# Two quarters of a tile per program step in a fused attention and LoRA-mixture kernel

## The reference

```python
x = x + xattn(layernorm(x), ctx, ctx)      # x, ctx: (8, 512, 2048) float32
x = x + ffn(layernorm(x), router_w, A, B)
# xattn: 8 heads of 64 of the 512 channels; q = softmax over the channels of a head,
#        k = softmax over the 2048 positions; kvs = k.T @ v per head; out = q @ kvs
# ffn:   logits = x @ router_w.T (4 experts), the two best kept, softmax over them = gates
#        mid = x @ A.T (rank 16 per expert), delta = gates * (mid @ B.T) * 4
```

## Time and profile before

| what | value |
|---|---|
| median of 3 runs | 462.5 us (462.09 to 462.72) |
| the profiled execution | 461.86 us, its span 460.1 us |
| mean granted TensorE clock | 0.968 |
| PE, DVE, ACT, POOL busy | 94%, 82%, 69%, 78% of the span |
| moved by DMA | 137.55 MB, 299 GB/s |

### The profile page before, as it was taken

The page is one execution under the profiler, slowest core; times in us unless marked ns, Lnnn a source line. Parts: engine busy times, 40 slices in busy tenths (PEclk is TensorE's granted clock), DMA queues, the critical chain, the costliest instruction groups (busy, mean ns, idle before and its releaser), DMA issues.

```text
span 460.1 us, 16033 instructions
## 1 busy us (share of the span) xinstructions
PE 434.0 (94%) x6504; PEld 382.7 (83%) x6504; DVE 378.9 (82%) x1045; ACT 317.8 (69%) x436; POOL 358.7 (78%) x343
## 2 busy tenths in 40 slices
PE   6569998999999999999999999999999999999975
PEld 5458887888889888888888988888888988888854
DVE  2478778898998989898988989898989989775864
ACT  1266888795858777786858777786958687785320
POOL 0457999988898989898898988898888989894510
PEclk9658999999999999999999999999999999999997
DMA  8995997799999999999999999999999997445247
GB/s 288 420 410 187 310 274 266 261 285 322 347 285 355 327 342 345 312 336 320 339 305 323 338 361 334 323 326 328 355 291 345 300 366 256 172 170 184 93 182 275
DMA packets 38969, 137.55 MB, mean 299 GB/s; under 512 B 4208, under 2 KB 6384, under 8 KB 38768
## 3 DMA queue, kind: packets, MB, share of 16 engines
q1 hardware_dynamic: 38896, 136.52, 85.8%
HBM read 102.95 MB, written 33.55 MB: 297 GB/s over the span
## 4 chain that ended last, share of the span: by engine, by line
PE 80%; POOL 6%; DVE 4%; DMA 4%; issue 2%; ACT 2%; SPq 1%; POOLq 0%; DVEq 0%
PE num_ps L407 23%; PE kv_ps L390 15%; PE raw_ps L423 12%; PE delta_ps L478 11%; PE delta_ps L479 6%; PE kv_ps L438 5%; PE raw_ps L454 4%; DMA sq_a<-in_bt_dram 4%; POOL ek_sb L311 3%; POOL y_sb L323 3%; PE kv_ps L443 1%; PE raw_ps L464 1%; DVE max_n L632 1%; DVE y_sb L716 1%; PE kv_ps L375 1%
## 5 line engine op out<-in xcount | busy, mean ns | idle before, releaser
L311 POOL TENSOR_TENSOR ek_sb<-ctx_sb,kmax_row 128x512 f32<-128x512 f32 x128 | 167.6, 1311 | 35.7 <-ACT kmax_row L511 35.7
L323 POOL TENSOR_TENSOR y_sb<-attnT,y_sb 128x512 f32<-128x512 f32 x128 | 164.0, 1281 | 38.6 <-DVE attnT L707 38.5
L407 PE MATMUL num_ps<-kv_sb,x_sb 128*128 128x130 f32 x1024 | 140.8, 281 | 3.3 <-ACT kv_sb L563 2.0
L407 PEld LDWEIGHTS num_ps<-kv_sb,x_sb 128*128 128x128 f32 x1024 | 125.7, 192 | 6.2 <-ACT kv_sb L563 2.7
L716 DVE TENSOR_TENSOR y_sb<-delta_ps,y_sb 128x512 f32<-128x512 f32 x128 | 87.5, 684 | 23.3 <-PE delta_ps L479 22.1
L632 DVE TENSOR_REDUCE max_n<-ctx_sb 128x32 f32<-128x512 f32 x128 | 86.4, 677 | 10.6 <-DMA ctx_sb<-in_ctxt_dram 10.6
L390 PE MATMUL kv_ps<-ctx_sb,ek_sb 128*64 128x65 f32 x2048 | 93.2, 234 | 0.2 <-ACT ek_sb L533 0.2
L707 DVE TENSOR_TENSOR attnT<-num_ps,rden 128x512 f32<-128x512 f32 x128 | 88.5, 691 | 4.8 <-DVE rden L704 0.4
L390 PEld LDWEIGHTS kv_ps<-ctx_sb,ek_sb 128*64 128x64 f32 x2048 | 74.6, 140 | 17.8 <-issue 6.0
L533 ACT ACTIVATE ek_sb<-ek_sb 128x1024 f32<-128x1024 f32 x64 | 67.2, 1049 | 25.8 <-POOL ek_sb L311 25.7
L423 PE MATMUL raw_ps<-w_sb,y_sb 128*64 128x69 f32 x2048 | 84.4, 223 | 0.0
(11 more groups left out here) (67 smaller groups left out, 461.7 us busy)
## 6 DMA issues: line engine op xcount, KB each, us to landing
ctx_sb<-in_ctxt_dram SPq DMA_DIRECT2D x64, 520.0 KB, 5.6
x_sb<-in_x_dram SPq DMA_DIRECT2D x64, 512.0 KB, 6.1
y_sb<-in_xt_dram SPq DMA_DIRECT2D x64, 512.0 KB, 6.5
out_dram<-y_sb SPq DMA_DIRECT2D x60, 512.0 KB, 6.3
out_dram<-y_sb SPq DMA_DIRECT2D x8, 256.0 KB, 3.8
sq_a<-in_bt_dram SPq DMA_DIRECT2D x1, 1024.0 KB, 16.2
w_sb<-in_wt_dram SPq DMA_DIRECT2D x1, 552.0 KB, 10.1
cst<-in_consts_dram SPq DMA_DIRECT2D x1, 145.0 KB, 2.3
```

The costliest lines, as they stand in the source:

```text
L311: pool.tensor_tensor(ek_sb[:, t % 2, chunks(g), :].rearrange("p (a b) c -> p a b c", b=2), ctx_sb[:, t % 4, 2 * g:2 * g + 2, 1:P + 1, :].r ...
L323: pool.tensor_tensor(y, attnT[:, g, :], y, ALU.add).then_inc(x1_made, 1)
L407: mm = pe.matmul(num_ps[:, j // 2, at:at + 2 * (DH + 1)], x_sb[:, t % 4, c * P:(c + 1) * P], kv_sb[:, t % 2, :], start=True, stop=True, sk ...
```

## The change

Every engine's loop now goes over `q` in steps of 2, and each operation handles two quarters in one step. On TensorE the two `numerator` calls, which need the array as 128 columns, stand with the two `delta` calls, `sum_squares`, `turn_mid` and `spread_kmax` between them; then come both `kv`, then both `project` (64 columns), then `fold_squares` (32 columns). `delta_ps` is one pair of banks that both deltas of a step fill, and one `add_delta` of twice the width reads. `turn_max` writes into `delta_ps`, no longer into `num_ps`, so `delta` waits for `kmax_made` and `turn_max` for `out_made`. `max_part` handles 64 rows at a time. `fold_squares` adds the 16 blocks of squares into one block of 128 columns, so `copy_squares` copies 128 columns where it copied 384, and `sum_squares` is one matmul where it was three. Offsets grow by one where they were odd. The orders of VectorE, ScalarE and GpSimd are written anew.

```diff
@@ TensorE @@
-            for q in range(FIRST, LAST + 1):
+            for q in range(FIRST, LAST + 1, 2):
+                turn_max(tile_in(q, -4))
+                numerator(*tile_at(q, 6))
                 delta(*delta_at(q))
-                turn_max(q)
-                sum_squares(q)
-                if q == 1:
+                delta(*delta_at(q + 1))
+                sum_squares(tile_in(q, 12))
+                turn_mid(pair_in(q, 20))
+                if q == 2:
                     sum_w()
-                numerator(*tile_at(q, 5))
-                spread_kmax(q)
-                kv(*tile_at(q, 0))
-                project(*tile_at(q, 7))
-                fold_squares(q)
-                turn_mid(q)
+                spread_kmax(tile_in(q, -4))
+                numerator(*tile_at(q + 1, 6))
+                for k in range(2):
+                    kv(*tile_at(q + k, 0))
+                for k in range(2):
+                    project(*tile_at(q + k, 8))
+                fold_squares(tile_in(q, 10))
@@ delta @@
-                after(pe, out_made, 8 * p + i - 1)
+                if i % 2 == 0:
+                    after(pe, out_made, 4 * p + i // 2)
+                    after(pe, kmax_made, min((8 * p + i + 22) // 4 + 2, NT))
@@ VectorE @@
+            for q in range(FIRST, LAST + 1, 2):
+                a, b = pair_in(q, 16), pair_in(q, 18)
+                kv_recip(tile_in(q, 4))
+                max_whole(tile_in(q, -4))
+                ln1_mean(tile_in(q, -2))
+                normalise(*tile_at(q, 6))
+                add_delta(*delta_at(q))
+                normalise(*tile_at(q + 1, 6))
+                mid_low(pair_in(q, 20))
...
+                max_part(*tile_at(q, -8))
...
+                for k in range(2):
+                    bn_part(*tile_at(q + k, -4))
...
@@ add_delta @@
-                y = y_sb[:, pair_slots(p), 2 * i:2 * i + 2, :]
+                y = y_sb[:, pair_slots(p), 2 * i:2 * i + 4, :]
@@ SP, the last pair @@
-            for i in range(8):
-                sp.wait_ge(out_made, 8 * (NP - 1) + i + 1)
+            for i in range(4):
+                sp.wait_ge(out_made, 4 * (NP - 1) + i + 1)
                 store_last(i)
```

More of the change, by code:

```diff
@@ L120, in xattn_lora_moe_kernel @@
         num_ps = bank("num_ps", (P, 2, 512))
[L121 to L122 removed]
+        delta_ps = bank("delta_ps", (P, 2, 512))
+        max_ps = delta_ps[:, 0, 0:P]
         ctx_landed = [sem(f"ctx_landed{i}") for i in range(4)]
@@ L452, in sum_squares, with turn_mid @@
                 pe.wait_ge(sq_summed, t + 1)
-                for k in range(3):
-                    mm = pe.matmul(raw_ps[p % 2][:, odd, COL_SQ:COL_SQ + 2], sq_sum[:, t % 2, k, :], ones[:, 0:2],
-                                   start=False, stop=(k == 2), skip_group_check=True)
-                mm.then_inc(sq_done, 1)
-            def turn_mid(q):
-                p = pair_at(q, 15)
+                pe.matmul(raw_ps[p % 2][:, odd, COL_SQ:COL_SQ + 2], sq_sum[:, t % 2, :], ones[:, 0:2],
+                          start=False, stop=True, skip_group_check=True).then_inc(sq_done, 1)
+            def turn_mid(p):
                 if p is None:
@@ L808, in mid_low @@
                                   ALU.subtract).then_inc(lo_made, 1)
-            for q in range(FIRST, LAST + 1):
-                early = q < 0
-                if early:
-                    max_whole(q)
-                a, b, c = pair_at(q, 13), pair_at(q, 14), pair_at(q, 15)
-                if b is not None:
-                    gate_beats(b, 0)
-                if c is not None:
-                    gate_mid(c)
-                max_part(*tile_at(q, -8))
-                kv_recip(q)
+            for q in range(FIRST, LAST + 1, 2):
+                a, b = pair_in(q, 16), pair_in(q, 18)
[6 more added lines that the diff above has]
+                mid_low(pair_in(q, 20))
                 if a is not None:
@@ L823, in _ @@
                 if b is not None:
-                    gate_beats(b, 1)
-                    gate_mask(b)
-                mid_low(q)
-                bn_part(*tile_at(q, -5))
-                add_delta(*delta_at(q))
+                    gate_rank(b)
+                max_part(*tile_at(q, -8))
                 if a is not None:
                     gate_logits(a)
-                if b is not None:
-                    gate_rank(b)
-                if not early:
-                    max_whole(q)
-                normalise(*tile_at(q, 5))
-                if a is not None:
                     gate_below(a)
+                    gate_beats(a, 0)
+                    gate_beats(a, 1)
+                    gate_mask(a)
                 if b is not None:
```

183 lines of the change are left out of this document (83 added, 100 removed).

## The result

| | before | changed |
|---|---|---|
| median of 6 runs each, same chip | 462.47 us (461.86 to 462.72) | 467.79 us (467.01 to 468.67) |
| ratio to before, 95% interval | | 1.0117 (1.0102 to 1.0131) |
| span of the profiled execution | 460.1 us | 465.2 us |
| mean granted TensorE clock | 0.968 | 0.951 |

The change made the kernel 1.2% slower. I had forecast 0.4% faster, 460.7 us.

The account below looks back on a forecast made before the run. TensorE was taken to set the pace before the change. Start 87, 13 pairs of 25.0, 22.0 to the last fold and 24.6 behind it gave a 458.6 us span, forecast as 460.7 us; range 451 to 468, its own 453 to 461.5.

Parts of the forecast that it names:

- S: Moment VectorE begins a step's first normalise; the second numerator was to start 1.07 us later, TensorE standing about 0.3.
- step B: Second of a pair's four steps, with the gates' second half on VectorE; 6.45 us there, 6.5 by TensorE.
- the two lists: TensorE's and VectorE's work per step; the longer sets its length: 5.6, 6.5, 6.4, 6.5, together 25.0 us per pair.
- D: Fourth step of a pair, with two bn_stats, kv_recip and max_whole on VectorE: 6.1 us there, 6.5 by TensorE.
- second rival: Steady part: VectorE's lateness passed on through the one num_ps; slower, 468 us at a pair of 25.6; chance 0.30.
- Step C: Third step of a pair, with mid_low and two bn_stats; VectorE's list 6.1 us, 6.4 with deltas starting late.
- the guard: Deltas' wait for max_whole (kmax), since turn_max writes into delta_ps; deltas 0.3 us late after a step that fills VectorE.
- A: First step of a pair, with the gates' first half and ln1_mean; VectorE's list rules at 5.6 us.
- Start: Up to normalise 16: first normalise at about 38 us, steady part at 87 instead of 81.86, 5 us lost.
- End: Behind the last fold: one-copy delta_ps makes four rounds of 2.5 us each; 24.6 us counted, 21.0 before.
- Rival 1: Steady part: TensorE alone sets the pace, VectorE ready early; 443 to 445 us; chance 0.17.
- Rival 3: Whole kernel: steady part gains what start and end lose (5+1.7 us), at a pair of 25.1; 462 us; chance 0.16.

Follow-up runs that it names:

- e8: Changed kernel plus a needless one-input VectorE maximum over 256 columns, four per pair of tiles; 483.04 us, ratio 1.0443.
- e9: Kernel before plus the same needless one-input VectorE maximum over 256 columns, four per pair of tiles; 468.29 us, ratio 1.0133.
- e7: Changed kernel with maximum in the second delta bank, b_lo one step earlier, and two delta banks in turn for the last pair; 452.55 us, ratio 0.9787.
- e4: Kernel before with only the new squares: one block of 128 columns, one matmul in sum_squares instead of three; 456.49 us, ratio 0.987.
- e10: Changed kernel with the old squares: blocks of 384 and 128 columns, three matmuls in sum_squares; 480.86 us, ratio 1.0393.
- e1: Changed kernel with turn_max writing into the second bank of delta_ps, so only the second delta of a step waits for the maximum; 460.39 us, ratio 0.997.
- e3: Changed kernel with two delta_ps banks used in turn, 512-column additions and half-size stores, for the last pair alone; 462.20 us, ratio 1.0.
- e2: Changed kernel with the four b_lo pieces computed one step earlier on VectorE (q = 2, not 4); 466.03 us, ratio 1.0068.
- e11: Three-repair version (452.55 us) with both kv ahead of the second numerator and the wide maximum ahead of the second normalise; 459.04 us, ratio 0.9924.
- e5: Changed kernel plus a needless VectorE addition of 256 columns with two SBUF inputs, four per pair of tiles; 505.43 us, ratio 1.0942.
- e6: Kernel before plus the same needless VectorE addition of 256 columns, four per pair of tiles; 475.60 us, ratio 1.0285.

## Why the prediction was wrong

- **What bounds it, and the mechanism: right.** The wait of the second numerator for `attnT` arose where I put it, at S+0.97 in step B for my S+1.07, and a step lasts as long as the longer of the two lists. e8 against e9 shows that the changed kernel passes on nine tenths of VectorE's lateness, the one before under four tenths. It appears 33 times with 24.4 us, where I wrote some 50 times; in the steady part it stands in B and D only. My sign for the second rival, TensorE waiting more than 2 us per pair, did not come: PE stands 1.4.
- **The widths: right.** A wide addition lasted 1.22 us and a wide maximum 1.21; from start to start a maximum took 1.13, and the addition 1.14 where the next operation waited for nothing. The overhead of 0.07 in these terms came from no row. The runs bear it out: 0.33 for 256 columns (e8), 0.60 for 512, 1.13 for 1024.
- **TensorE's saving: somewhat smaller.** PE was busy for 23.69 us of a pair in e7, for my 23.3 (my terms, 25.65 less 1.4 and 0.8, add to 23.45). The squares took 0.7 us from it (24.92 in e4) for my 0.8, the new order 0.8 (e10) to 1.2 (e4 to e7) for my 1.4. What it was worth depended on the guard: nothing with it, 0.54 us per pair without (e1 against e4). That most of it would stay in the new wait was the right sentence; I still credited the pair with 0.64 us, and it was 0.43.
- **Step C and the guard: the term of the steady part that was mis-sized.** For the guard I took 0.3 us, in C alone. Against e1 it cost 0.48 there (6.74 for 6.26) and 0.13 in A, where I counted nothing for it: 0.6 per pair, twice what I had. Without the guard my lists give 24.7 per pair, and e1 shows 24.73, but by errors that cancel: C was 6.26 for my 6.1, where `ln1_var` (0.17) was not in my list, and B and D were 0.05 shorter each. So twelve pairs took 25.31 for my 25.0, and the last 23.95, which I had not foreseen; 12x0.31 less 1.05 are the 2.7 us by which the steady part missed.
- **Start: mis-sized.** I had 87 and it was 90.09. The first `normalise` (38.59 for my 38; `b_lo` took 3.5 us for 4.2, and the maximum ahead of it began 0.6 later than I had) and the first step (8.33 for 8.3) held. The second step took 6.81 for my 5.4, because the clock had fallen and I had given it the fast one; the six steps behind it took 36.4 for 35.6. The numerator of that second step shows the clock, in the timeline of PE:

```profile
47.89 2.10 PE L411 MATMUL num_ps<-kv_sb,x_sb 128*128 128x130 f32 x8
49.92 1.71 PE L395 MATMUL kv_ps<-ctx_sb,ek_sb 128*64 128x65 f32 x32
51.47 1.14 PE L427 MATMUL raw_ps<-w_sb,y_sb 128*64 128x69 f32 x32
```

  The 2.23 us in which PE stood before `spread_kmax` at 47.50, for `copy_kv`, cost little by themselves, as VectorE's S was at 46.92 and the numerator had to wait for it until about 47.9. But then the numerator took 2.03 us to the next start for 0.99, and both `kv` 1.55 for 0.98: 1.6 us, all of the excess of this step. These are places of one execution: in e3 and e8, whose start up to there is the same program, `normalise` 16 came at 91.4 and 91.3.
- **End: right in sum, by luck.** 24.6 forecast, 25.2 measured. The four last rounds took 2.53 at the fast clock and 3.39 at the slow one, and three of them had the slow one. I had named this ("up to 1 us per step") and left it out of the sum; three times 0.86 is 2.6 us. All else behind the last fold was 2 us shorter than the 14.6 that my sum leaves for it and that I had not split into terms. One part of it the rows show: from the end of the last addition to the end of the span it is 3.2 us, for 4.8 before, though the last store has twice the size. Why is not shown.
- **The sum.** 3.1 (start), 2.7 (pairs), 0.2 and 0.6 (end) are the 6.6 us between my 458.6 and the 465.2 of the span. A pair of 25.1 was the point from which I let the second rival decide, and 25.21 is beyond it; of its 468 only 2.7 of the 6.6 us came from there, though, and the rest from start and end, while I had worked it out from a pair of 25.6 alone. That its time came out is luck. My own last step was off as well: 460.4 and the 0.6 to the median are 461.0, not 460.7. The lists of B and D add to 6.33 and 6.03, for which I wrote 6.45 and 6.1; TensorE's 6.5 is longer, so the sum does not change.
- **Rival 1** (TensorE alone, 443 to 445) is refuted by the waits for `attnT` and by e8, in which work on VectorE alone made a pair 1.2 us longer. **Rival 3** (a pair of 25.1 that pays for start and end) had the right signs; start and end lost 10.7 us together (8.2 and 2.5), where it had 6.7.

The theory with which I went into the experiments stands: e7 got 15.2 us back, as much as the three places gave one by one. Its rival, that undoing one would only move the wait, holds for e2 in small (0.46 us of a new wait), and for e11.

What stays open: how much of e11's loss is the round trip and how much the keys, what the pads would cost without the guard, and why the old order passes on nearly four tenths of a pad (that VectorE was busy for 23.1 of 25.65 us there fits, but no run took it apart).

## What to carry to other kernels

Before work is grouped on the busiest engine, look for what the old order hid: with one copy of a buffer between two engines, lateness is passed on as soon as nothing stands between its two uses (nine tenths here, under four tenths with `kv` and `project` between them). A guard added for a reused buffer is to be followed through all that the late instruction releases, not only to the first: here it took in every pair what the new order had gained. And cost the start and the end of a kernel at the clock that its gaps may bring: here a numerator at 0.50 took 2.03 us for 0.99, and a round of the end 3.39 for 2.53.

## What the runs showed of the hardware

A VectorE addition of 256 columns with both inputs in SBUF lasted 0.42 us with GpSimd idle and 1.20 to 1.42 us when it began during one of GpSimd's additions or subtractions (e5; 1.02 in e6), and ended 0.3 us behind that one; the maximum with one input lasted 0.41 at every place, with GpSimd busy 22.4 of 26.5 us. The Trainium skill, SBUF — State Buffer, section "Who interferes with whom", says that a VectorE instruction with two SBUF inputs contends with a GpSimd instruction that reads SBUF; it calls the shared port pair an exclusive lock and says that the order of issue decides who blocks. The trace agrees. The wide additions of this kernel have one input in PSUM and showed nothing of it (1.22 us each, 64 times).

The clock fell in the middle of the start too, where TensorE had plenty to do directly behind: PE was busy for 0.27 us from 45 to 46, did nothing from 46 to 47 and was busy for 0.4 from 47 to 48, and from 48 to 51, busy all the time, it was granted 0.50, which is 1.2 GHz. The windows of the changed kernel:

```profile
46.00:47.00 1.00, 0.00 (x0) 0.00 (x0) 0.94 (x5) 0.29 (x1) 0.00 (x0) 1.00 0.73 300
...
48.00:49.00 1.00, 1.00 (x5) 1.00 (x6) 0.00 (x0) 0.97 (x3) 1.00 (x1) 0.50 0.07 16
```
